# A graph layer's edge gather: more tiles taken from a float32r table on TensorE, fewer by indirect transfer

## The chip, the cores and the metric

The kernel runs on one core of one Trainium2 chip. The metric is the device time of one execution in microseconds (us); it is read from timed runs, and beside them there is one profiled execution. The engines are PE (TensorE), DVE (VectorE), ACT (ScalarE), POOL (GpSimd) and SP (SyncE, which here only issues transfers).

## What is computed

A graph has 3125 nodes with 128 features each (x) and 53125 edges, sorted by their target node (dst), each with 64 features. Cut to what matters:

```
h   = concat([x[src], edge_attr], axis=1)            # 53125 x 192
h   = relu(batchnorm(h @ W1 + b1, g1, be1))          # statistics over all edges
agg = segment_mean(h, dst, 3125)                     # per target node
h2  = relu(batchnorm(concat([x, agg]) @ W2 + b2, g2, be2))
out = layernorm(x + relu(h2 @ Wl + bl))
```

The product is split: `h @ W1` is `(x @ W1x)[src] + edge_attr @ W1e`. The first part is a table of one row per node, of which each edge needs the row of its source node.

## The kernel before

**Phase one** goes over the edges once and keeps every pre-activation row in SBUF (`res`; the fourth group of each cycle goes to DRAM, `spill_out`). A *tile* is 128 edges x 128 features, a *group* is four tiles (q = 0 to 3), a *cycle* (i = 0 to 25) four groups. The node table `x @ W1x` is made at the start, kept in SBUF (`ysb`) and written to DRAM (`ytab`). For every group PE makes the edge product (`product`, L744), GpSimd gathers the table's rows with one indirect transfer per tile (`gather`, L660), and DVE adds the two (`make_h`, L1230). DVE then adds the group to a running sum (`sum_h`, L1251) and ACT's squares of it to another (`sum_sq`, L1258), for the batch norm. Once a cycle DVE makes one-hots of the target nodes (`onehots`, L1209), PE counts them (`counts`, L809), ACT places the counts (`place_counts`, L1012), and in cycles 1 to 14 PE also makes a piece of `x @ W2` (`x_product`, L817), which needs the turned x (`xt0`) in `res`.

**The third group (q = 2) is special.** Two of its four tiles in cycles 2 to 15, and one in cycles 16 to 19, are not gathered but selected on PE: DVE writes one-hots in bfloat16 of which of 3125 nodes each edge wants (`node_onehots`, L1243, five pieces of 125 x 1280 or 125 x 640), PE multiplies 25 blocks of `ysb` in float32 with them (`node_rows`, L757), ACT copies the turned result (`rows_out`, L1039), and PE turns it back onto the edge product (`rows_back`, L765). From cycle 20 all sixteen tiles are gathered.

**Phase two** goes over the kept rows: after the batch-norm chain (L1324 to L1340) DVE takes `max(h, -u)` (`maxes`, L1355), PE sums windows of target nodes with the one-hots (`window_sum`, L890), ACT and GpSimd add them up. It reads the rows from `res` and, for the fourth groups, from DRAM. The node part (`x`, mean, W2, layer norm) follows.

The order of work is written by hand: each engine runs its own list in order and waits on semaphores. GpSimd may start gathering a group once `make_h` of the group four before is done. PE may make a product once `make_h` of the group four before is done. Each transfer of SP's queue waits its turn behind those that stand before it.

Of the kernel before, what the change touches and what calls it, by code (L numbers as in the profile page):

```python
# [27 lines left out]
BF16 = mybir.dt.bfloat16  # L28
I32 = mybir.dt.int32
# [9 lines left out]
U = 4  # L39
# [6 lines left out]
ROWS0 = 2  # L46
ROWS1 = 20
PAIRS1 = 16
NODEQ = 2

def node_tiles(i):

    return 2 if ROWS0 <= i < PAIRS1 else 1 if ROWS0 <= i < ROWS1 else 0

def gnn_kernel(nc, E, x, xt, src, src_rows, dst, dst_rows, ea, W1, b1, g1, be1, W2, b2, g2, be2, Wl, bl, out):
# [8 lines left out]
    YROWS = 25 * P  # L66
# [10 lines left out]
    XLOADS = [BATCH[0:1], BATCH[1:2], BATCH[2:4], BATCH[4:]]  # L77
    YSAVES = [BATCH[0:2], BATCH[2:4], BATCH[4:6], BATCH[6:]]

    ytab = nc.dram_tensor("ytab", (YROWS, F), F32, kind="Internal").ap()  # L80
    h2x_dram = nc.dram_tensor("h2x_dram", (P, H2, N), F32, kind="Internal").ap()
    spill = nc.dram_tensor("spill", (NI, P, TILES * F), F32, kind="Internal").ap()
    rc_dram = nc.dram_tensor("rc_dram", (N,), F32, kind="Internal").ap()
# [3 lines left out]
    with ctx:  # L87
# [9 lines left out]
        GF = TILES * F  # L97
        res = sb("res", [P, NI * KEEP * GF])
# [23 lines left out]
        nodeid = sb("nodeid", [P, NT])[:, :]  # L122
        rowst_sb = sb("node_rows_turned", [P, 2 * P])
# [14 lines left out]
        TAB = 16 * (len(CUTS) * len(YSAVES) + 1)  # L138
# [13 lines left out]
        ysb = tail(NT * F)  # L152
        NODES = range(ROWS0, ROWS1)
        NODEAT = [P * sum(node_tiles(m) for m in range(i)) for i in range(ROWS1 + 1)]
        srcz = tail(NODEAT[-1] // 2).bitcast(BF16)
        TAB0 = at
        xt0 = tail(N)
        XT0 = at
        dsti = tail(TILES * NG)
# [6 lines left out]
        zeros = tail(F)  # L166
# [34 lines left out]
        XP = 20  # L201
        XW = XP * NT
        XSTEPS = [(h, k, min(XP, PN - k)) for k in range(0, PN, XP) for h in range(H2)]
# [12 lines left out]
        psP = [psH[0], psH[1], psT[0], psC[1]]  # L216
# [3 lines left out]
        nodep = psC[0][0:PN, (U + 1) * WIN:(U + 1) * WIN + NT]  # L220
        NODECUT = [(t, t + 5) for t in range(0, NT, 5)]
        NB5 = len(NODECUT)
        NODEROWS = 12
        srcn = res[:, NODEROWS * KEEP * GF:NODEROWS * KEEP * GF + NODEAT[-1]]
        LONE = TAB0 - NT * P
        lone_hot = res[:, LONE:TAB0]
        pair_hot = res[:, LONE - 2 * NT * P:LONE]
        assert LONE - 2 * NT * P >= PAIRS1 * KEEP * GF and LONE >= ROWS1 * KEEP * GF
        assert NODEROWS * KEEP * GF + NODEAT[-1] <= PAIRS1 * KEEP * GF

        def node_chunk(i, b):

            t0, t1 = NODECUT[b]
            w = node_tiles(i) * P
            return (pair_hot if i < PAIRS1 else lone_hot)[0:PN, t0 * w:t1 * w]

        PRODUCTS = [(0, q) for q in range(U)] + [(1, 0)]
        for i in range(1, NI):
            order = [(i, 1), (i, 2), (i, 3)] + ([(i + 1, 0)] if i + 1 < NI else [])
            PRODUCTS += order if i not in NODES else order[1:] + order[:1]  # L240
# [7 lines left out]
        psK = [psT[1], psC[0], psH[0]]  # L248
# [10 lines left out]
        s_srcb = sem("src_rows_spread")  # L259
        s_srcz = sem("src_rows_less_partition")  # L260
# [3 lines left out]
        rows_kept = sem("node_rows_turned_copied")  # L264
        rows_added = sem("node_rows_added")
# [11 lines left out]
        s_zr = sem("zeros_ready")  # L277
# [86 lines left out]
        def slot(i, par, q):  # L364

            return resg(i, q) if q < KEEP else away[par]
# [90 lines left out]
        def _(sp):  # L457
# [1077 lines left out]
```

## Time and profile before

| | |
|---|---|
| timed runs, median of 3 | 635.34 us (634.62 to 635.60) |
| span of the profiled execution (its time on the page; no other time of it is given) | 631.8 us |
| median less span | 3.5 us |
| busy: PE, DVE, ACT, POOL | 503.7, 464.6, 201.2, 403.6 us |
| phase one, up to the first `maxes` | 496.1 us |
| from there to the end | 135.7 us |

The busy times are shares of a span with very different stages, so no engine's total says what bounds it; the section of rows has the stages apart. A float32 matmul stands in the trace as two MATMUL and two LDWEIGHTS instructions; a bfloat16 matmul stands as one each.

### The profile page before, as it was taken

To read this page: it belongs to the slowest core of one execution; us is meant where nothing else is said; L and a number is where in the kernel's file an instruction comes from. 1 tells how busy PE (TensorE), PEld (TensorE's weight loads), DVE (VectorE), ACT (ScalarE), POOL (GpSimd) and SP (SyncE) were. 2 spreads that over 40 slices of the span, in tenths; PEclk is the share of its full clock that TensorE was granted. 3 is DMA by queue.
4 is the path that set the end of the run, shared out by engine and by line. 5 is a ranking of instruction groups with operands and counts; after the bars stand their busy time and mean duration, and the time that the engine had idled before them with its cause. 6 is when DMAs were issued, how large, how long until landed. Compare 5 with 4: busy or idle time off the path is not lost.

```text
span 631.8 us, 9631 instructions
## 1 busy us (share of the span) xinstructions
PE 503.7 (80%) x2681; PEld 412.7 (65%) x2681; DVE 464.6 (74%) x720; ACT 201.2 (32%) x537; POOL 403.6 (64%) x507
## 2 busy tenths in 40 slices
PE   4749999999999999997866634444456899999984
PEld 4637778777777778886664422222223799999674
DVE  4789988888888998987666454454444777777786
ACT  2242222222222222222211211121114566666475
POOL 4777777777777777777777777777777133333500
PEclk9879999999999999999777755555557999999997
DMA  7953344434443434444334342334224277777103
GB/s 202 324 167 121 115 135 135 137 117 138 137 122 116 126 111 138 126 121 121 102 119 121 87 150 78 96 118 121 85 70 120 74 235 228 223 237 231 33 2 101
DMA packets 47608, 84.35 MB, mean 133 GB/s; under 512 B 11721, under 2 KB 23288, under 8 KB 47447
## 3 DMA queue, kind: packets, MB, share of 16 engines
q1 hardware_dynamic: 28834, 47.98, 23.6%
q0 software_dynamic: 12288, 25.19, 15.9%
q10 hardware_dynamic: 6453, 10.79, 4.8%
q8 instruction: 15, 0.25, 0.2%
q14 instruction: 18, 0.15, 0.1%
HBM read 63.82 MB, written 20.08 MB: 133 GB/s over the span
## 4 chain that ended last, share of the span: by engine, by line
PE 53%; POOL 24%; issue 9%; DVE 8%; DMA 3%; ACT 1%; SPq 1%; POOLq 0%; ACTq 0%; DVEq 0%
PE psH L757 25%; POOL res L660 17%; PE psH L890 7%; PE psC L890 7%; POOL work L660 7%; PE psH L744 4%; PE psT L817 3%; PE psT L744 2%; PE psC L744 2%; DVE res L1230 2%; DMA work<-ytab,srci 2%; DVE res L1387 1%; PE psT L809 1%; DMA w1x<-in_L_gnn_W 1%; DVE res L1243 1%
## 5 line engine op out<-in xcount | busy, mean ns | idle before, releaser
L660 POOL DMA_INDIRECT res<-ytab,srci x268 | 253.9, 947 | 81.7 <-issue 79.5
L757 PE MATMUL psH<-res 125*128 125x256 f32 (+1 forms) x900 | 178.7, 359 | 7.0 <-DVE res L1230 7.0
L757 PEld LDWEIGHTS psH<-res 125*128 125x128 f32 x900 | 154.9, 191 | 28.0 <-DVE res L1230 10.7
L660 POOL DMA_INDIRECT work<-ytab,srci x104 | 98.2, 944 | 31.7 <-issue 31.4
L1243 DVE TENSOR_TENSOR res<-res,psC 125x1280 f32<-125x1280 bf16 (+1 forms) x90 | 116.8, 1333 | 0.8 <-ACT res L1030 0.8
L744 PE MATMUL psH<-w1e,work 128*128 128x256 f32 x200 | 69.0, 480 | 42.8 <-DVE res L1230 42.8
L984 ACT ACTIVATE agg<-res 128x512 f32<-128x512 f32 x78 | 49.1, 630 | 143.7 <-DVE res L1230 80.5
L1230 DVE TENSOR_TENSOR res<-psH,res 128x512 f32<-128x512 f32 x50 | 34.5, 689 | 76.5 <-DMA res<-ytab,srci 48.6
L1355 DVE TENSOR_TENSOR work<-res,psX 128x512 f32<-128x512 f32 x103 | 70.2, 687 | 19.5 <-PE psC L890 12.2
L744 PEld LDWEIGHTS psH<-w1e,work 128*128 128x128 f32 x200 | 44.4, 239 | 56.5 <-issue 42.5
L685 POOL TENSOR_TENSOR agg<-agg,srci 128x64 f32 x104 | 32.0, 308 | 70.9 <-ACT srci L1095 70.0
L1258 DVE TENSOR_TENSOR psX<-agg,psX 128x512 f32<-128x512 f32 x103 | 71.0, 689 | 0.0
L1251 DVE TENSOR_TENSOR psS<-res,psS 128x512 f32<-128x512 f32 x78 | 54.3, 696 | 2.7
L890 PE MATMUL psH<-work 128*128 128x128 f32 (+1 forms) x416 | 50.8, 275 | 1.5 <-DVE work L1355 1.5
L890 PE MATMUL psC<-work 128*128 128x128 f32 (+1 forms) x416 | 50.7, 275 | 0.0
L890 PEld LDWEIGHTS psH<-work 128*128 128x128 f32 x416 | 48.5, 192 | 1.9 <-DVE work L1355 1.2
L744 PE MATMUL psC<-w1e,work 128*128 128x256 f32 x100 | 32.7, 458 | 21.0 <-DVE work L1230 21.0
L890 PEld LDWEIGHTS psC<-work 128*128 128x128 f32 x416 | 48.5, 192 | 0.0
L744 PEld LDWEIGHTS psT<-w1e,work 128*128 128x128 f32 x100 | 22.2, 232 | 40.1 <-DVE res L1230 25.0
L744 PE MATMUL psT<-w1e,work 128*128 128x256 f32 x100 | 33.1, 462 | 16.4 <-DVE res L1230 13.4
L744 PEld LDWEIGHTS psC<-w1e,work 128*128 128x128 f32 x100 | 21.5, 226 | 30.0 <-DVE work L1230 27.0
L984 ACT ACTIVATE agg<-work 128x512 f32<-128x512 f32 x25 | 15.7, 630 | 77.5 <-DVE work L1230 77.5
(200 smaller groups left out, 518.7 us busy)
## 6 DMA issues: line engine op xcount, KB each, us to landing
work<-in_edge_attr SPq DMA_DIRECT2D x26, 512.0 KB, 3.7
spill<-work SPq DMA_DIRECT2D x26, 256.0 KB, 2.3
res<-spill SPq DMA_DIRECT2D x25, 256.0 KB, 3.1
res<-ytab,srci POOLq DMA_INDIRECT x268, 2.5
hot_dram<-hotb ACTq DMA_DIRECT2D x13, 256.0 KB, 2.7
hot_dram<-work ACTq DMA_DIRECT2D x13, 256.0 KB, 2.4
hotb<-hot_dram SPq DMA_DIRECT2D x13, 256.0 KB, 2.7
work<-hot_dram SPq DMA_DIRECT2D x13, 256.0 KB, 3.0
```

What stands on the lines that cost most here:

```text
L660: pool.indirect_dma_start(rows[:, j * F:(j + 1) * F], None, ytab, bass.IndirectOffsetOnAxis(ap=srci[:, j, g:g + 1], axis=0)).then_inc(gath ...
L685: pool.tensor_tensor(w, w, wsum[:, q, :], ALU.add).then_inc(agg_added, 1)
L744: last = pe.matmul(psP[q][:, b * 2 * F:(b + 1) * 2 * F], ea_cols(par, q, b), w1e[:, :, :].rearrange("p a f -> p (a f)"), start=(b == 0 or ...
L757: last = pe.matmul(psP[1][:, 0:w], ysb[0:PN, t * F:(t + 1) * F], node_chunk(i, b)[:, k:k + w], start=(t == 0), stop=(t == NT - 1))
L817: pe.matmul(psT[1][:, 0:n * NT].rearrange("o (p t) -> o p t", t=NT), w2x[:, h * P:(h + 1) * P], xtv[:, :, k:k + n].rearrange("f t p -> f p ...
L890: last = pe.matmul(psA[q][:, 0:n], mx[:, q, j * F:(j + 1) * F], hotf[:, q, j * WIN:j * WIN + n], start=(j == 0), stop=(j == TILES - 1))
L984: act.activation(sq[g % 2], slot(i, i % 2, q), ACT.Square).then_inc(sq_ready, 1)
L1230: dve.tensor_tensor(h, psP[q][:, :], h, ALU.add).then_inc(h_ready, 1)
L1243: dve.tensor_tensor(node_chunk(i, b).rearrange("p (t e) -> p t e", t=t1 - t0), srcz[0:PN, NODEAT[i]:NODEAT[i] + w].unsqueeze(1).broadcast_ ...
L1251: last = dve.tensor_tensor(psS[:, :], slot(i, par, q), psS[:, :], ALU.add)
L1258: last = dve.tensor_tensor(psX[:, :], sq[g % 2], psX[:, :], ALU.add)
L1355: dve.tensor_tensor(tiles(mx[:, q, :]), tiles(hin), negu, ALU.max).then_inc(m_ready, 1)
```

## The change

All four tiles of the third group are now selected on PE, in every cycle from 2 to 25; twelve of sixteen tiles are gathered. The table is laid out as 112 partitions x 28 rows (3136 rows, node = 28 p + t) and kept in two float32r halves: `tab_hi` is ACT's copy of `ysb`, `tab_lo` is `ysb - tab_hi`, made by DVE (`table_low`). A node number is split in three: its upper part names one of 112 x 7 cells of four rows (SPAN = 4, STEPS = 7), its lower two bits one of the four. The upper parts (`srcr`, keys) are made by DVE, written to DRAM, and spread over 112 partitions per cycle (`load_keys`). For each tile DVE compares 112 x 896 (`node_onehot`), PE runs 14 matmuls of 512 moving columns (7 steps x high and low, `node_tile`), which leave all four candidate rows of each edge in one PSUM bank, ACT copies the first (`node_first`), and DVE overwrites it where the edge wants the second, third or fourth (`node_pick`, three predicated copies of 128 x 128). Tiles of cycle i + 1 are selected during cycle i.

PSUM: two banks hold edge products (`psP`) where four did, so `product` waits for `make_h` of the group two before; two banks hold candidates (`psN`).

SBUF: the halves and one-hots lie where the rows of cycles 18 to 25 were. These go into the place of cycles 0 to 7 (`home`), whose rows are first written to `spill_all` (8 x 768 KB) and, when the last pick is done, read back by SP (`back_all`); DVE waits for all of it before phase two. `place` gives the cycle's place in phase two.

```diff
+            def load_keys(i):
+                if i - 2 in NODES:
+                    sp.wait_ge(nhot_ready, node_nth(i - 2, NODET - 1) + 1)
+                sp.dma_start(keys[i % 2][0:TP, :], key_dram[i - NODE0, :].partition_broadcast(TP)
+                             ).then_inc(keys_in[i % 2], 16)
...
+                if i < SWAP:
+                    sp.dma_start(spill_all[i, :, :], res[:, i * KEEP * GF:(i + 1) * KEEP * GF]).then_inc(spilled_all, 16)
...
+            sp.wait_ge(node_rows, (SPAN - 1) * NODEALL)
+            sp.wait_ge(spilled_all, 16 * SWAP)
+            for i in range(SWAP):
+                k = place(i, NI) * KEEP * GF
+                sp.dma_start(res[:, k:k + KEEP * GF], spill_all[i, :, :]).then_inc(back_all, 16)
...
-                for j in range(node_tiles(i) if q == NODEQ else 0, TILES):
+                for j in range(NODET if q == NODEQ and i in NODES else 0, TILES):
...
-                pe.wait_ge(h_ready, g - U + 1)
+                pe.wait_ge(h_ready, g - 1)
...
+            def node_tile(i, j):
+                n = node_nth(i, j)
+                pe.wait_ge(nhot_ready, n + 1)
+                if n >= 2:
+                    pe.wait_ge(node_rows, (SPAN - 1) * (n - 1))
+                for a in range(STEPS):
+                    k = (j * STEPS + a) * P
+                    for part, table in enumerate((tab_hi, tab_lo)):
+                        last = pe.matmul(psN[n % 2][:, :], nhot[0:TP, k:k + P],
+                                         table[0:TP, a * SPAN * F:(a + 1) * SPAN * F],
+                                         start=(a == 0 and part == 0), stop=(a == STEPS - 1 and part == 1))
+                last.then_inc(nhot_used, 1)
...
+                act.wait_ge(nhot_used, n + 1)
+                act.activation(node_slot(i, j), psN[n % 2][:, 0:F], ACT.Copy).then_inc(first_of_four, 1)
...
+                dve.tensor_tensor(nhot[0:TP, j * STEPS * P:(j + 1) * STEPS * P].rearrange("p (a e) -> p a e", a=STEPS),
+                                  keys[i % 2][0:TP, j * P:(j + 1) * P].unsqueeze(1).broadcast_to([TP, STEPS, P]),
+                                  nodep.unsqueeze(2).broadcast_to([TP, STEPS, P]), ALU.is_equal).then_inc(nhot_ready, 1)
...
+                dve.copy_predicated(node_slot(i, j), pick[:, b - 1, j, place(i, NI):place(i, NI) + 1].broadcast_to([P, F]),
+                                    psN[n % 2][:, b * F:(b + 1) * F]).then_inc(node_rows, 1)
...
+                    dve.tensor_tensor(tab_lo[0:TP, cut], ysb[0:TP, cut], tab_hi[0:TP, cut].bitcast(F32), ALU.subtract
+                                      ).then_inc(s_lo, 1)
...
+            dve.wait_ge(back_all, 16 * SWAP)
```

PE's list, in one cycle of the middle (cycle 11) before; `psH <- res` at L757 is `node_rows`, with five pieces of five matmuls:

```order
239 L757 MATMUL psH<-res 128x256 [waits node_onehots_ready]
240 L757 MATMUL psH<-res 128x256 x4
241 L757 MATMUL psH<-res 128x256 [waits node_onehots_ready]
242 L757 MATMUL psH<-res 128x256 x4
243 L817 MATMUL psT<-res,agg 128x500 [waits cnt_rows_placed]
244 L744 MATMUL psT<-w1e,work 128x256 [waits h_ready]
...
246 L744 MATMUL psC<-w1e,work 128x256 [waits h_ready]
...
248 L744 MATMUL psH<-w1e,work 128x256 [waits h_ready,ea_loaded1]
...
250 L809 MATMUL psT<-hotb,onesb 128x256 [waits w2_x_copied,cnt_rows_placed,hotb_ready]
...
252 L744 MATMUL psH<-w1e,work 128x256 [waits h_ready,node_rows_turned_copied]
...
254 L765 MATMUL psT<-ident,node_rows_turned 128x128 [waits node_rows_turned_copied]
```

The same list after the change, from the third product of a middle cycle on; behind row 412 stand the 28 matmuls of two tiles (rows 413 to 440), and 14 each stand behind 442 and 458:

```order
406 L863 MATMUL psT<-res,agg 128x504 [waits cnt_rows_placed]
407 L792 MATMUL psH<-w1e,work 128x256 [waits h_ready]
...
409 L855 MATMUL psT<-hotb,onesb 128x256 [waits w2_x_copied,cnt_rows_placed,hotb_ready]
...
411 L792 MATMUL psT<-w1e,work 128x256 [waits h_ready,ea_loaded1]
412 L792 MATMUL psT<-w1e,work 128x256
...
441 L792 MATMUL psH<-w1e,work 128x256 [waits h_ready]
442 L792 MATMUL psH<-w1e,work 128x256
...
457 L792 MATMUL psT<-w1e,work 128x256 [waits h_ready]
458 L792 MATMUL psT<-w1e,work 128x256
```

The selection now stands in four pieces between the products, and the first product of the next cycle stands behind the counts and ahead of the last two tiles.

DVE's list before, from the third group of a middle cycle to the next cycle's first; L1243 is `node_onehots`:

```order
294 L1227 TENSOR_TENSOR res<-psT,res 128x256 [waits node_rows_added,gathered1_2,ea_product_ready]
295 L1228 COPY res<-psT 128x256
296 L1251 TENSOR_TENSOR psS<-res,psS 128x512 [waits h_ready]
297 L1258 TENSOR_TENSOR psX<-agg,psX 128x512 [waits squares_ready]
298 L1243 TENSOR_TENSOR res<-res,psC 125x640 [waits node_onehots_used]
299 L1230 TENSOR_TENSOR work<-psC,work 128x512 [waits gathered1_3,ea_product_ready]
300 L1251 TENSOR_TENSOR psS<-work,psS 128x512 [waits h_ready]
301 L1258 TENSOR_TENSOR psX<-agg,psX 128x512 [waits squares_ready]
302 L1243 TENSOR_TENSOR res<-res,psC 125x640 [waits node_onehots_used] x2
303 L1230 TENSOR_TENSOR res<-psH,res 128x512 [waits gathered0_0,ea_product_ready]
```

DVE's list after, from the fourth group (`make_h` at L1291) to the next cycle's first; L1314 is `node_pick`, L1302 `node_onehot`:

```order
403 L1291 TENSOR_TENSOR work<-psH,work 128x512 [waits gathered1_3,ea_product_ready]
404 L1328 TENSOR_TENSOR psS<-work,psS 128x512 [waits h_ready]
405 L1314 COPY_PREDICATED res<-res,psH 128x128 [waits node_rows_picked,node_rows_first_of_four]
406 L1335 TENSOR_TENSOR psX<-agg,psX 128x512 [waits squares_ready]
407 L1314 COPY_PREDICATED res<-res,psH 128x128 [waits node_rows_picked,node_rows_first_of_four]
408 L1302 TENSOR_TENSOR node_onehots<-res,psC 112x896 [waits node_onehots_used]
409 L1314 COPY_PREDICATED res<-res,psH 128x128 [waits node_rows_picked,node_rows_first_of_four]
410 L1302 TENSOR_TENSOR node_onehots<-res,psC 112x896 [waits node_onehots_used]
411 L1314 COPY_PREDICATED res<-res,psC 128x128 [waits node_rows_picked,node_rows_first_of_four] x3
412 L1302 TENSOR_TENSOR node_onehots<-res,psC 112x896 [waits node_onehots_used]
413 L1291 TENSOR_TENSOR res<-psT,res 128x512 [waits gathered0_0,ea_product_ready]
```

Three one-hots and six picks now stand between the sums of the fourth group and the next cycle's first `make_h`, where two pieces of one-hots stood.

## Rows read from the trace of the kernel before

**Rows 1.** The page: busy time and share of each engine.

```profile
PE 503.7 (80%) x2681; PEld 412.7 (65%) x2681; DVE 464.6 (74%) x720; ACT 201.2 (32%) x537; POOL 403.6 (64%) x507
```

**Rows 2.** The page's groups by line: busy, mean ns, idle before.

```profile
L660 POOL DMA_INDIRECT res<-ytab,srci x268 | 253.9, 947 | 81.7 <-issue 79.5
L660 POOL DMA_INDIRECT work<-ytab,srci x104 | 98.2, 944 | 31.7 <-issue 31.4
```

**Rows 3.** Windows: length, busy time per engine, PE clock, DMA share, GB/s.

```profile
47.00:290.00 243.00, 238.25 (x1071) 193.76 (x1072) 219.27 (x267) 60.62 (x142) 183.88 (x195) 1.00 0.42 126
400.00:488.00 88.00, 44.08 (x99) 24.52 (x97) 41.05 (x60) 18.86 (x45) 66.44 (x71) 0.54 0.33 97
496.00:591.00 95.00, 93.57 (x836) 93.44 (x836) 73.31 (x108) 55.63 (x206) 31.67 (x103) 1.00 0.70 207
```

**Rows 4.** Timeline of PE, one middle cycle: start, duration, instruction.

```profile
205.53 11.06 PE L757 MATMUL psH<-res 125*128 125x256 f32 x50 [0.34 <-DVE res L1230]
216.42 2.04 PE L817 MATMUL psT<-res,agg 128*128 128x500 f32 x2
218.28 1.05 PE L744 MATMUL psT<-w1e,work 128*128 128x256 f32 x4
...
220.89 0.60 PE L809 MATMUL psT<-work,onesb 128*128 128x256 bf16 x4
221.33 1.03 PE L744 MATMUL psH<-w1e,work 128*128 128x256 f32 x4
...
223.14 11.06 PE L757 MATMUL psH<-res 125*128 125x256 f32 x50 [0.34 <-DVE res L1230]
```

**Rows 5.** Timeline of DVE in the same cycle.

```profile
204.78 0.69 DVE L1230 TENSOR_TENSOR res<-psH,res 128x512 f32<-128x512 f32 x1 [1.65 <-PE psH L744]
205.51 0.70 DVE L1251 TENSOR_TENSOR psS<-res,psS 128x512 f32<-128x512 f32 x1
206.11 0.69 DVE L1258 TENSOR_TENSOR psX<-agg,psX 128x512 f32<-128x512 f32 x1
206.71 1.22 DVE L1209 TENSOR_TENSOR work<-psC,loc 128x1024 bf16<-128x1024 f32 x1
207.84 0.41 DVE L1227 TENSOR_TENSOR res<-psT,res 128x256 f32<-128x256 f32 x1
...
209.82 1.48 DVE L1243 TENSOR_TENSOR res<-res,psC 125x1280 f32<-125x1280 bf16 x1
211.22 0.68 DVE L1230 TENSOR_TENSOR work<-psC,work 128x512 f32<-128x512 f32 x1
```

**Rows 6.** Timeline: copies of 128 columns out of PSUM on two engines.

```profile
296.78 0.28 ACT L1039 ACTIVATE node_rows_turned<-psH 128x128 f32<-128x128 f32 x1
...
310.83 0.28 DVE L1228 COPY res<-psT 128x128 f32<-128x128 f32 x1
```

**Rows 7.** Timeline of DVE: first groups of cycles 2 and 25, last group, phase two.

```profile
57.34 0.68 DVE L1230 TENSOR_TENSOR res<-psH,res 128x512 f32<-128x512 f32 x1
...
475.22 0.69 DVE L1230 TENSOR_TENSOR res<-psH,res 128x512 f32<-128x512 f32 x1 [3.07 <-DMA res<-ytab,srci]
...
490.32 0.69 DVE L1230 TENSOR_TENSOR work<-psC,work 128x512 f32<-128x512 f32 x1 [1.19 <-DMA work<-ytab,srci]
...
496.13 1.88 DVE L1355 TENSOR_TENSOR work<-res,psX 128x512 f32<-128x512 f32 x3 [0.52 <-PE psX L878]
```

**Rows 8.** Windows with busy DMA engines (last two columns: DMA share, GB/s).

```profile
9.00:13.00 4.00, 4.00 (x19) 4.00 (x20) 2.47 (x6) 0.99 (x2) 2.92 (x3) 1.00 0.97 333
...
28.00:30.00 2.00, 2.00 (x15) 1.82 (x14) 1.97 (x4) 0.63 (x1) 1.39 (x3) 1.00 1.05 420
...
505.00:585.00 80.00, 80.00 (x718) 80.00 (x718) 61.72 (x91) 48.87 (x180) 27.39 (x90) 1.00 0.77 230
```

**Rows 9.** The page's DMA issues: size, us from issue to landing.

```profile
spill<-work SPq DMA_DIRECT2D x26, 256.0 KB, 2.3
```

More of the change, by code:

```diff
@@ L28 @@
 BF16 = mybir.dt.bfloat16
+F32R = mybir.dt.float32r
 I32 = mybir.dt.int32
@@ L97, in gnn_kernel, with shared @@
         GF = TILES * F
+        AREA = (NI - SWAP) * KEEP * GF
+        with ExitStack() as low:
+            def shared(name, cols, dt=F32R):
+                return low.enter_context(nc.sbuf_tensor(name, [P, cols], dt))
+            shared("below_node_area", AREA, F32)
+            tab_hi = shared("table_high", TT * F)
+            tab_lo = shared("table_low", TT * F)
+            nhot = shared("node_onehots", NODET * STEPS * P)
         res = sb("res", [P, NI * KEEP * GF])
@@ L150, in tail @@
             return res[:, at:at + n]
[L152 to L157, printed above, removed]
+        NODES = range(NODE0, NI)
+        keys = [tail(NODET * P) for _ in range(2)]
+        pick = tail((SPAN - 1) * NODET * NI).bitcast(I32).rearrange("p (b j s) -> p b j s", b=SPAN - 1, j=NODET)
+        assert at >= AREA + 2 * TT * F + NODET * STEPS * P
+        at = AREA
+        xt0 = tail(YROWS)
         XT0 = at
+        ysb = tail(TT * F)
+        srcr = tail(NODET * P)[0:len(NODES), :]
+        low2 = tail(NODET * NI).bitcast(I32).rearrange("p (j s) -> p j s", j=NODET)
         dsti = tail(TILES * NG)
@@ L761, in rows_back @@
-            def rows_back(i):
-                pe.wait_ge(rows_kept, i - ROWS0 + 1)
-                for j in range(node_tiles(i)):
-                    last = pe.matmul(psP[NODEQ][:, j * F:(j + 1) * F], rowst_sb[:, j * P:(j + 1) * P], ident[:, :],
-                                     start=False, stop=(j == node_tiles(i) - 1))
-                last.then_inc(rows_added, 1)
+            def node_tile(i, j):
+                if i not in NODES or j >= NODET:
+                    return
+                n = node_nth(i, j)
+                pe.wait_ge(nhot_ready, n + 1)
+                if n == 0:
+                    pe.wait_ge(s_hi, len(YBATCH))
+                    pe.wait_ge(s_lo, len(YBATCH))
+                if n >= 2:
[7 more added lines that the diff above has]
+                last.then_inc(nhot_used, 1)
@@ L859, in stay_awake @@
                 for _ in range(n):
[L860 removed]
+                    pe.matmul(psC[1][:, 0:P], ident[:, :], ident[:, :], start=True, stop=True)
             stay_awake(3)
```

343 lines of the change are left out of this document (190 added, 153 removed).

## The prediction

> **What bounds the kernel now.** I read the page's busy times first [rows 1]: no engine is near the whole span, so the stages must be told apart. The windows do that [rows 3]: from 47 to 290 us PE is busy 238 of 243 us at the full clock, from 400 to 488 us half of the time at 0.54 of it, and in phase two again nearly always. GpSimd's gathers are the other candidate: 372 of them to the table, each about 0.945 us long with 0.30 us of issue before it [rows 2], (253.9 + 81.7) / 268 = 1.252 us each, 465 us in all, one after the other. So the number of gathered tiles sets the cycle wherever PE is not slower: 14 tiles make 17.5 us, 15 make 18.8, 16 make 20.0. In cycles 2 to 14 PE needs just as long: its period is 223.14 - 205.53 = 17.61 us with 0.34 us idle [rows 4]. Both engines are at the limit there; afterwards GpSimd alone is, and it is the sum of both that the span shows: from the first `make_h` of cycle 2 to that of cycle 25, 475.22 - 57.34 = 417.9 us, 18.2 per cycle [rows 7]. After that come 20.9 us to the first `maxes` at 496.13 (the last four groups' gathers, then the batch-norm chain, 5.8 us behind the last `make_h` at 490.32), then 135.7 us of phase two and the node part.
>
> **GpSimd.** 96 tiles leave its list where 32 had, so 64 transfers go. Twelve tiles make 15.0 us per cycle. It may run four groups ahead of `make_h` as before, so if another engine is slower than 15.0, GpSimd waits and costs nothing.
>
> **PE.** Per cycle 56 matmuls of 512 columns in float32r come in; `node_rows` and `rows_back` go. No row shows float32r. The nearest rows: a float32 matmul of 256 columns is two instructions of 10.89 / 50 = 0.218 us [rows 4], so 0.87 us for 512 columns; bfloat16 takes 0.44 / 4 = 0.110 us for 256 columns, so 0.22 for 512. Below 0.22 lies nothing, since both come to one column per cycle of the full clock (a float32 matmul then being four passes). The bounds are 0.22 and 0.87; I take 0.218, one pass, because the kernel multiplies by a high and a low half itself, which is what several passes would do inside. Loads of 128 columns stay hidden: in phase two PE alternates load and half matmul 836 times each in 95 us, 0.114 us a pair [rows 3], well under 0.218.
> So a tile takes 14 x 0.218 = 3.05 us and four take 12.2. With four products at 2.61 / 3 = 0.87, the counts 0.44 and the piece of `x @ W2` 1.86 [rows 4] that is 12.2 + 3.5 + 0.4 + 1.9 = 18.0 us in cycles 1 to 12, and 16.1 from cycle 15 on (13 and 14 have a short piece). PE is slower than the gathers throughout.
>
> **DVE.** Spacings rather than durations count, since instructions overlap by about 0.09 us [rows 5]: 0.73 for `make_h` with the wait of `sum_h` on it, 0.60 each for the sums, 1.13 for the 1024-element one-hots. Per cycle that is 4 x 1.93 + 1.13 = 8.85. The five pieces of 1280 (211.22 - 209.82 = 1.40 each) leave. Four of 896 elements come: 1.40 x 896 / 1280 = 0.98, say 1.0 each, 4.0. Twelve predicated copies of 128 columns come, which no row shows: a plain copy of that size lasts 0.28 [rows 6], 0.20 spaced; if the mask or the old value costs a second reading it is 0.33 spaced, and twice over 0.45. I take 0.20 to 0.27 (it moves the same elements as the plain copy) and add 0.13 where a pick waits on the one before (the last three, and a few others). That is 2.4 to 3.2 plus 0.6. In sum DVE works about 16.2 us a cycle, against 8.85 + 7.0 = 15.9 before: more, and now with a hand-over in both directions at each tile.
>
> **How the two meet.** I lay the lists side by side with t = 0 at the end of a cycle's last tile on PE. PE: product 0.9, tile 3.9, product 4.8, tile 7.9. DVE cannot pick before ACT's copy of 0.28 [rows 6], so its first pick starts at 4.4; then pick, sum, pick, sum, pick and the one-hots, 2.9 us, bring it to 7.3, `make_h` of the second group is done at 8.0, of the third at 10.0. PE's fourth product waits for the one and the next cycle's first for the other. With the x piece PE is at 9.7 by itself and needs neither wait: the two tiles end at 18.0, period 18.1. Without it PE waits until 8.1 and 10.1, makes products and counts to 11.0, and the tiles end at 17.1: period 17.2. From cycle 2 to cycle 25 that makes 11 x 18.1 + 12 x 17.2 = 405.5, less about 2 because cycle 24 makes no one-hots: 403.5 us, against 417.9. **14.4 us are gained.**
>
> **The start.** Seven pieces of `table_high` on ACT, seven of `table_low` at 0.60, 4.2 us, and four one-hots, 4.0, fall into cycle 0 of DVE, and some 3.4 us of short list work ahead of it. Much hides behind the twenty gathers up to cycle 1's end (25 us of GpSimd), but PE's first tile waits for the low half. Followed through, the first `make_h` of cycle 2 comes at about 60 instead of 57.3: **2.7 us lost** (bounds 0 and 8). The 8 writes of 768 KB hide in cycles whose DMA share is 0.42 [rows 3]; the two row moves (keys) are small and come a cycle early.
>
> **The read-back.** It starts only at the last pick, just ahead of the first `make_h` of cycle 25. 8 x 786 KB = 6.29 MB. With all engines busy the trace moves 333 to 420 GB/s [rows 8]; in phase two, with smaller rows, 230 at 0.77. I take 360: 17.5 us, plus 2 of latency (a 256 KB write needs 2.3 to land [rows 9]), plus 0.6 because the first one-hots stand behind it in SP's queue: `maxes` 20 us after cycle 25's first `make_h`. What else must happen there: 10 us for the groups now that gathers wait ready, counts and folds beside it, the products of the last group with itself, the chain: about 18.5. So the read-back ends last, by little, and the tail is 20 against 20.9. **0.9 us gained**, of which I give 0.8 to a colder start of PE. Phase two does the same work, 135.7.
>
> **The sum.** 60 + 403.5 + 20 + 0.8 + 135.7 = 620 us of span, against 631.8; with the 3.5 us between span and median, **624 us**.
>
> **Rivals.**
> *DVE becomes the bound (slower, 0.18).* Place: the predicated copies. DVE's cycle is 13.5 + 12 c; with c over 0.38 it passes PE's 18.1. At 0.45 the cycle is about 18.3 to 19.1, and the lists followed through give 26 us more, 650. It decides against the change from about 0.36 on. For it: no such instruction is in the trace, and it has three operands. Against it: TENSOR_TENSOR with two operands is no slower per element than COPY [rows 5, 6].
> *Hand-overs cost more than I gave them (slower, 0.10).* Each tile passes PE, ACT, DVE and back; another 0.7 us per cycle is 16 us, 640. Speaking for it: products have half the PSUM they had.
> *float32r needs two or four passes (slower, 0.06).* 1344 matmuls at 0.436 give about 905 us, at 0.87 about 1490.
> *The read-back is slow (0.07).* At 230 GB/s it takes 27.4 us, 10 more: 634, about no change.
> *PE is faster than its columns (faster, 0.03).* If consecutive matmuls of 512 columns overlapped, PE and DVE would fall under GpSimd's 15.0 us; 23 cycles of that are 345 instead of 403.5, 566 us. Against it stands that bfloat16 comes at one column per clock in rows 4; DVE's 16.2 forbids half of it too, leaving some 595.
> The Trainium skill (TensorE: Matmul & The Clock Gate, Back-to-back issue gap) gives about 131 ns per 512-column matmul as sustained; the trace's 0.110 us for 256 columns disagrees.
> *My forecast* has the rest, 0.56, from 614 to 633.
>
> **Chances and range.** A measurement of this kernel can tell some 0.2%, 1.3 us. Faster: 0.56 + 0.03 + 0.03 of the slow read-back, 0.62. Same: the other 0.04 of it. Slower: 0.18 + 0.10 + 0.06 = 0.34. The range 613 to 650 leaves out the passes, PE's overlap and the worst of DVE.
>
> **What would show it.** L810 MATMUL spaced 0.218 us; L1314 at 0.28 to 0.35 long; 1.25 us gathers with idle before them "<-DVE"; periods of 18.1 and 17.2; DVE's first `maxes` released by DMA `spill_all`. Wrong if L1314 is over 0.45, if PE shows gaps over 1.5 us per cycle, or if L810 is not one pass.

## The result, and the profile after

The changed kernel takes 643.01 us (median of 4 runs, 642.42 to 644.37), the kernel before 634.98 us (634.38 to 635.60) on the same chip: a ratio of 1.0133, 95% interval 1.0117 to 1.0149. It is slower by 8.0 us, where the prediction had it faster by 11; 643 lies inside the range of 613 to 650, on the side that was held less likely. The profiled execution took 643.24 us, its span is 641.5.

The page of the changed kernel: busy times, the chain that ended last by engine, and the costliest groups (to be held against [rows 1] and [rows 2]):

```profile
PE 591.4 (92%) x3067; PEld 485.9 (76%) x3067; DVE 510.9 (80%) x1015; ACT 215.3 (34%) x621; POOL 344.3 (54%) x442
...
PE 76%; DVE 14%; issue 4%; DMA 3%; ACT 1%; SPq 1%; DVEq 0%; ACTq 0%; POOL 0%; POOLq 0%
...
L709 POOL DMA_INDIRECT res<-ytab,srci x204 | 193.0, 946 | 111.8 <-DVE res L1291 53.7
...
L1302 DVE TENSOR_TENSOR node_onehots<-res,psC 112x896 fp32r<-112x896 f32 x96 | 103.4, 1079 | 0.0
L1314 DVE COPY_PREDICATED res<-res,psH 128x128 f32<-128x128 int32 x144 | 42.7, 296 | 59.8 <-ACT res L1087 59.7
```

GpSimd lost 59 us of work and now idles "<-DVE res L1291", that is, for `make_h`; it stands with 0% on the chain. PE gained 88 us of work and holds 76% of the chain. Windows of the changed kernel (length, busy time per engine, PE clock, DMA share, GB/s) say where:

```profile
60.00:290.00 230.00, 229.25 (x978) 177.86 (x976) 187.73 (x356) 58.80 (x159) 139.94 (x148) 1.00 0.47 145
300.00:480.00 180.00, 175.54 (x780) 141.36 (x780) 152.86 (x293) 42.42 (x122) 116.26 (x124) 1.00 0.39 114
...
490.00:495.00 5.00, 4.90 (x25) 3.22 (x25) 2.72 (x5) 4.43 (x7) 0.00 (x0) 1.00 1.01 424
495.00:500.00 5.00, 4.06 (x37) 3.87 (x36) 2.15 (x12) 3.67 (x5) 0.00 (x0) 1.00 1.01 415
500.00:505.00 5.00, 0.69 (x3) 0.50 (x4) 1.15 (x3) 1.03 (x3) 0.00 (x0) 0.82 0.48 180
505.00:510.00 5.00, 5.00 (x25) 5.00 (x25) 4.46 (x6) 1.06 (x4) 0.62 (x2) 0.50 0.38 107
```

PE is busy 229.25 of 230 us where there are pieces of `x @ W2`, and 175.5 of 180 us in the later cycles, where before it had half of its time free [rows 3]. The span, stage by stage (us; the starts are those of DVE's `make_h` and of the first `maxes`; the forecast's 0.8 for a colder PE is put to phase two):

| stage | before | forecast | after |
|---|---|---|---|
| up to the first `make_h` of cycle 2 | 57.3 | 60 | 63.05 |
| from there to that of cycle 25 | 417.9 | 403.5 | 418.8 |
| from there to the first `maxes` | 20.9 | 20 | 22.1 |
| phase two and the node part | 135.7 | 136.5 | 137.6 |
| span | 631.8 | 620 | 641.5 |

The 418.8 us are eleven cycles of 18.43 on average (2 to 12; one is 18.78 and the next 18.08), one of 17.56, one of 23.73 (cycle 14), nine of 17.54 to 17.64 and a last one of 16.54. Three pieces of the timeline carry the rest. PE at the start of a middle cycle's tiles, in the changed kernel:

```profile
202.07 0.39 PE L810 MATMUL psH<-table_high,node_onehots 112*128 112x512 f32 x1
202.30 0.40 PE L810 MATMUL psH<-table_low,node_onehots 112*128 112x512 f32 x1
...
204.81 0.39 PE L810 MATMUL psC<-table_high,node_onehots 112*128 112x512 f32 x1
...
207.99 1.03 PE L792 MATMUL psH<-w1e,work 128*128 128x256 f32 x4
```

Float32r is one pass: from 204.81 to 207.99 fourteen matmuls take 3.18 us, 0.227 each (the 0.39 us of each overlap). Cycle 14, all engines:

```profile
288.98 0.54 PE L863 MATMUL psT<-res,agg 128*128 128x112 f32 x2
289.56 0.28 ACT L1087 ACTIVATE res<-psH 128x128 f32<-128x128 f32 x1 [8.24 <-PE psT L863]
...
289.87 0.30 DVE L1314 COPY_PREDICATED res<-res,psH 128x128 f32<-128x128 int32 x1 [5.81 <-ACT res L1087]
...
290.30 0.94 POOL L709 DMA_INDIRECT res<-ytab,srci x1 [8.08 <-PE psT L863]
...
293.53 2.08 PE L792 MATMUL psH<-w1e,work 128*128 128x256 f32 x4 [4.01 <-DVE res L1291]
```

The last piece of `x @ W2` reads the turned x from the place in `res` that cycle 15's rows take next. It stands on PE behind two tiles. ACT's first copy of the next cycle, every pick behind it and GpSimd's gathers wait 8 us for it, and PE in its turn 4.0 us. The wait costs more than itself, for behind it PE works at the lower clock (0.50 in this window):

```profile
295.00:297.00 2.00, 2.00 (x8) 1.45 (x7) 2.00 (x6) 0.40 (x2) 1.40 (x2) 0.50 0.34 57
```

From 293.53 to the next tile's start at 297.61 two products and the counts take 4.1 us, where at the full clock and without a wait they take 2.1. Of the 6.1 us by which this cycle is longer than its neighbours some 3.6 are the longer wait and some 2.5 the clock. And the end of phase one, DVE and SP's queue:

```profile
481.83 0.68 DVE L1291 TENSOR_TENSOR res<-psT,res 128x512 f32<-128x512 f32 x1
...
499.92 0.16 DVE L1432 TENSOR_TENSOR col<-col 128x1 f32<-128x1 f32 x1
...
503.92 1.88 DVE L1448 TENSOR_TENSOR work<-res,psX 128x512 f32<-128x512 f32 x3 [3.85 <-DMA spill<-work]
```
```profile
481.95 4.24 SPq L555 DMA_DIRECT2D res<-spill_all  x8
...
494.99 0.35 SPq L511 DMA_DIRECT2D spill<-work  x1
```

The chain is ready at 500.07, 18.2 us behind cycle 25's first `make_h`, as forecast (18.5). Then `maxes` waits 3.85 us, and what comes last is not the read-back but the last ordinary 256 KB write of `spill_out`: `maxes` overwrites `work`, from which it is read. The last read-back, the three loads that SP issued behind it and the write, with the time from issue to landing:

```profile
res<-spill_all SPq DMA_DIRECT2D x1, 768.0 KB, 15.4
hotb<-hot_dram SPq DMA_DIRECT2D x1, 256.0 KB, 11.4
work<-spill SPq DMA_DIRECT2D x1, 256.0 KB, 11.6
work<-hot_dram SPq DMA_DIRECT2D x1, 256.0 KB, 11.8
spill<-work SPq DMA_DIRECT2D x1, 256.0 KB, 8.5
```

Issued at 485.56, 490.25, 490.64, 491.11 and 494.99, they land at 500.95, 501.6, 502.3, 502.9 and 503.5. So the last read-back is there 0.9 us after the chain is ready; the other 2.6 us are the loads and the write that land behind it. PE starts after 4.31 us of idling at a granted clock of 0.50, which is the lower level, 1.2 GHz; its first 16 matmuls of phase two last 3.67 us.

### The profile page after: what moved, and what is told of

Same layout as the page of the kernel before. It is cut to its first block, busy times and chain, and to the rows that moved or that the text cites. A ratio compares the mean times of both kernels' runs of the same rounds, so it can differ in the third digit from the quotient of the medians.

```text
span 641.5 us, 11124 instructions
## 1 busy us (share of the span) xinstructions
PE 591.4 (92%) x3067; PEld 485.9 (76%) x3067; DVE 510.9 (80%) x1015; ACT 215.3 (34%) x621; POOL 344.3 (54%) x442
## 4 chain that ended last, share of the span: by engine, by line
PE 76%; DVE 14%; issue 4%; DMA 3%; ACT 1%; SPq 1%; DVEq 0%; ACTq 0%; POOL 0%; POOLq 0%
PE psH L810 24%; PE psC L810 18%; PE psH L933 8%; PE psC L933 7%; PE psT L792 6%; PE psH L792 5%; PE psT L863 3%; DVE res L1291 2%; DVE psX L1335 2%; DVE res L1314 2%; DMA spill<-work 1%; DVE work L1273 1%; PE psT L855 1%; DVE res L1480 1%; DVE hotb L1273 1%
## 5 line engine op out<-in xcount | busy, mean ns | idle before, releaser
L709 POOL DMA_INDIRECT res<-ytab,srci x204 | 193.0, 946 | 111.8 <-DVE res L1291 53.7
L810 PE MATMUL psH<-table_high,node_onehots 112*128 112x512 f32 x336 | 142.2, 423 | 4.6 <-DVE table_low L1322 4.6
L810 PE MATMUL psC<-table_high,node_onehots 112*128 112x512 f32 x336 | 135.5, 403 | 0.0
L810 PE MATMUL psH<-table_low,node_onehots 112*128 112x512 f32 x336 | 132.7, 395 | 0.0
L810 PE MATMUL psC<-table_low,node_onehots 112*128 112x512 f32 x336 | 131.0, 390 | 0.0
L1302 DVE TENSOR_TENSOR node_onehots<-res,psC 112x896 fp32r<-112x896 f32 x96 | 103.4, 1079 | 0.0
L1314 DVE COPY_PREDICATED res<-res,psH 128x128 f32<-128x128 int32 x144 | 42.7, 296 | 59.8 <-ACT res L1087 59.7
L810 PEld LDWEIGHTS psH<-table_high,node_onehots 112*128 112x128 f32 x336 | 64.3, 191 | 18.4 <-issue 5.0
L810 PEld LDWEIGHTS psH<-table_low,node_onehots 112*128 112x128 f32 x336 | 64.4, 192 | 13.4
L810 PEld LDWEIGHTS psC<-table_low,node_onehots 112*128 112x128 f32 x336 | 63.2, 188 | 13.1
L810 PEld LDWEIGHTS psC<-table_high,node_onehots 112*128 112x128 f32 x336 | 63.1, 188 | 13.1
```

The source lines that it names most:

```text
L709: pool.indirect_dma_start(rows[:, j * F:(j + 1) * F], None, ytab, bass.IndirectOffsetOnAxis(ap=srci[:, j, at:at + 1], axis=0)).then_inc(ga ...
L810: last = pe.matmul(psN[n % 2][:, :], nhot[0:TP, k:k + P], table[0:TP, a * SPAN * F:(a + 1) * SPAN * F], start=(a == 0 and part == 0), stop ...
L1302: dve.tensor_tensor(nhot[0:TP, j * STEPS * P:(j + 1) * STEPS * P].rearrange("p (a e) -> p a e", a=STEPS), keys[i % 2][0:TP, j * P:(j + 1) ...
L1314: dve.copy_predicated(node_slot(i, j), pick[:, b - 1, j, place(i, NI):place(i, NI) + 1].broadcast_to([P, F]), psN[n % 2][:, b * F:(b + 1) ...
```

## The experiments

Ratios are to the kernel before, on the same chip, with 95% intervals. Stages are read from the timeline as above.

**The x piece ahead of the tiles (e1_x_first).**

```diff
             def edge_step(i, par, nth):
+                if i == len(XSTEPS):
+                    x_product(i - 1)
                 product(i, par, nth, 1)
                 node_tile(i + 1, 0)
...
-                if i <= len(XSTEPS):
+                if i < len(XSTEPS):
                     x_product(i - 1)
```

> The last piece of x @ W2 (cycle 14) is made before that cycle's tiles instead of between the second tile and the third product. Theory A (ACT's first copy for cycle 15 and GpSimd's gathers for it wait for this piece, and that is the extra 6.2 us of the 23.73 us cycle in the changed kernel's trace): that cycle falls to 17.6, the time by 6 us, from 643 to 637. Rival (the long cycle comes from the clock of TensorE, which fell there, or from a late transfer, and the wait only stands beside it): the cycle stays above 22 us, the time at 642 to 644.

638.20 us (636.18 to 638.68), ratio 1.0064 (1.0046 to 1.0082). Cycle 14 takes 18.0 us instead of 23.7, and the other cycles do not move: the later ones stay at 17.6. The granted clock stays at 1.00 there (from 281 to 301 us), so its fall in the changed kernel came of the wait and was not the cause of the long cycle. PE now meets 0.45 us of waiting there instead of 4.01:

```profile
289.02 1.13 PE L792 MATMUL psH<-w1e,work 128*128 128x256 f32 x4
...
291.04 1.10 PE L792 MATMUL psT<-w1e,work 128*128 128x256 f32 x4 [0.45 <-DVE res L1293]
```

So some 5 of the 8 us by which the change lost are one wait, which stands in the diff's order and which I had not followed.

**The read-backs later, waited for later (e2_late_wait).** SP issues them behind the loads for phase two, and DVE waits for them only ahead of the 18th cycle of phase two, the first that needs one.

```diff
+            sp.wait_ge(node_rows, (SPAN - 1) * NODEALL)
...
+                sp.dma_start(res[:, k:k + KEEP * GF], spill_all[i, :, :]).then_inc(back_all, 16)
             spill_out(NI - 1, 1)
...
-                with dve.Fori(2, NI) as i:
+                with dve.Fori(2, NI - SWAP) as i:
+                    sum_step(i)
+                dve.wait_ge(back_all, 16 * SWAP)
+                with dve.Fori(NI - SWAP, NI) as i:
                     sum_step(i)
```

> The eight read-backs stand behind the first loads of phase two in SP's queue, and VectorE waits for them only before the 18th cycle of phase two, which is the first that needs them. Theory A (VectorE's 3.9 us wait for them, and the clock that falls in the idle time of TensorE before phase two, are all that they cost): first maxes at about 500.3 instead of 503.9, phase two at 135.7 instead of 137.6, in sum 5 us less: 638. Rival (their 6.3 MB cost as much wherever they lie, because phase two's own loads need the same transfer engines): phase two gets longer by 4 to 15 us, and the time stays at 642 or goes to 650.

648.83 us (646.83 to 649.84), ratio 1.0234 (1.0213 to 1.0255): slower by 6 us than the change itself. Theory A fell; the time lies where the rival had it, but not for the rival's reason, since phase two takes 137.0 us and the loss stands ahead of it. SP's queue and DVE in this kernel:

```profile
487.28 5.42 SPq L613 DMA_DIRECT2D res<-spill_all  x8
494.73 0.33 SPq L511 DMA_DIRECT2D spill<-work  x1
508.08 1.88 DVE L1447 TENSOR_TENSOR work<-res,psX 128x512 f32<-128x512 f32 x3 [8.26 <-DMA spill<-work]
```

The read-backs are issued 5.3 us later than in the change, and the 256 KB write lands 4.2 us later. The write is what `maxes` waits for. Whether the write is held by the queue's order or by busy DMA engines this run can't tell.

**The start in pieces (e3_pieces).** PE's first tile waits for each piece of the two halves, not for all.

```diff
-                if n == 0:
-                    pe.wait_ge(s_hi, len(YBATCH))
-                    pe.wait_ge(s_lo, len(YBATCH))
...
+                    if n == 0:
+                        pe.wait_ge(s_hi, a + 1)
+                        pe.wait_ge(s_lo, a + 1)
```

> TensorE's first tile waits for the low half of the table piece by piece, one of seven before each step, instead of for all seven. Theory A (the start is late because this tile begins at 40.3 us, 5 us after the first piece): it begins at about 36.5, the first make_h of cycle 2 comes at 59 to 60 instead of 63.05, time 640. Rival (VectorE's own list of 8 us, table_low and one-hots, sets the start): make_h of cycle 2 moves by under 1 us, time 642 to 643.

641.13 us (640.34 to 642.19), ratio 1.0109 (1.0088 to 1.0131). PE's first tile, in the changed kernel and in this one:

```profile
40.30 0.76 PE L810 MATMUL psH<-table_high,node_onehots 112*128 112x512 f32 x1 [4.58 <-DVE table_low L1322]
40.86 0.63 PE L810 MATMUL psH<-table_low,node_onehots 112*128 112x512 f32 x1
```
```profile
37.64 0.76 PE L810 MATMUL psH<-table_high,node_onehots 112*128 112x512 f32 x1 [0.88 <-DVE table_low L1322]
```

From cycle 0's first `make_h` to cycle 2's it takes 34.6 us (27.26 to 61.84) instead of 36.8 (26.22 to 63.05). That is 2.2 us less, and `make_h` of cycle 2 itself comes 1.2 us earlier, between what theory A and the rival had. The other runs that leave the start as the change has it take 35.8 to 36.8 us for this stretch; of the runs with this edit three take 34.6 and one (e8) 36.7. So the edit is worth some 1 to 2 us, but not in every execution. The medians differ by 1.9 us, the ratios by 1.5, and their intervals overlap.

**Half of PE's columns (e4_no_low).**

```diff
-                    for part, table in enumerate((tab_hi, tab_lo)):
+                    for part, table in enumerate((tab_hi,)):
```

> Leaves out the low half of the table: 7 instead of 14 matmuls per tile, so the selected rows are float32r-rounded. VectorE's and GpSimd's lists are untouched. Theory A (TensorE's list of 18.4 us is what a cycle lasts; behind it stands VectorE with about 16.2, then GpSimd with 15.0): TensorE needs 28 x 0.227 = 6.4 us less, cycles fall to 16.2, time about 598. Rival B (the chain tile, first copy, picks, next tile sets the cycle, whose length has more hand-overs than matmuls): cycles fall by 1 us at most, time above 620.

579.41 us (577.68 to 584.00), ratio 0.9150 (0.9102 to 0.9198). Most cycles take 15.33 us, below my 16.2 (cycle 14 takes 19.6), and the window shows what then bounds them:

```profile
257.00:410.00 153.00, 115.04 (x480) 85.15 (x480) 149.69 (x289) 45.07 (x122) 112.85 (x120) 0.98 0.45 134
```

DVE is busy 149.7 of 153 us, PE 115. So the limit of DVE's list is at most 15.3 us, not the 16.2 of the working, and in the changed kernel DVE has 2 to 3 us to spare in each cycle: PE was the bound.

**One predicated copy of three (e5_one_pick).** Two of the three `node_pick` of each tile are left out, and the counts that wait for them follow.

```diff
+PICKS = 1
...
-                if i not in NODES or j >= NODET:
+                if i not in NODES or j >= NODET or b < SPAN - PICKS:
```

> Leaves out two of the three predicated copies of every tile (the second and third candidate row are never taken), so 8 of 12 go per cycle; everything else stands. Theory A (TensorE's list is the bound): cycles 2 to 12 stay at 18.4, the later ones lose the waits of TensorE for make_h, 17.56 to about 17.0, time 634 to 640. Rival B (VectorE's list with its hand-overs is the bound): each cycle loses 8 x 0.2 = 1.6 us and the dependent waits, time about 605.

630.66 us (628.80 to 631.96), ratio 0.9939 (0.9918 to 0.9960). The cycles with an x piece stay at 18.43 to 18.44 us; the later ones go from 17.56 to 16.65. The window of later cycles:

```profile
325.00:425.00 100.00, 100.00 (x458) 83.26 (x457) 82.57 (x127) 24.98 (x72) 68.05 (x73) 1.00 0.44 125
```

PE is never idle there: 16.65 us is what its list takes by itself in a cycle without an x piece. In the first stretch PE alone sets the time in the changed kernel too; in the second its waits in the hand-overs between PE, ACT and DVE add 0.9 us. The time is below theory A's 634 because the later cycles lose 0.9 us instead of 0.6 and cycle 14 loses 2.3. The copies themselves last 0.295 us, as forecast; three that wait on one another take 1.10, which is 0.40 from one to the next, where the forecast had 0.33.

**Three tiles instead of four (e6_three).**

```diff
-NODET = 4
+NODET = 3
```

> Three tiles of the third group come from the table on TensorE instead of four, and GpSimd gathers thirteen of sixteen (one number changed, NODET = 3). Theory A (TensorE at 18.4 is the bound and has to lose a tile, 3.2 us): TensorE 15.2, VectorE 16.1 - 1.0 - 0.8 = 14.3, GpSimd 13 x 1.248 = 16.2, so cycles of 16.2 to 16.5 set by GpSimd, 23 of them 2 us shorter at the first eleven and 1.2 at the rest: time about 643 - 36 = 607, faster than the kernel before. Rival B (hand-overs set the cycle): the share of GpSimd's extra tile and the hand-overs add up, cycles above 17.3, time 630 or more.

596.43 us (595.79 to 597.66), ratio 0.9401 (0.9383 to 0.9419): 6% faster than before, and better than theory A's 607. Its gathers and a window of its later cycles:

```profile
L709 POOL DMA_INDIRECT res<-ytab,srci x228 | 215.4, 945 | 69.5 <-issue 66.7
```
```profile
320.00:430.00 110.00, 96.37 (x418) 74.00 (x416) 90.45 (x169) 27.52 (x75) 83.06 (x88) 1.00 0.43 124
```

Idle ahead of the gathers is nearly all issue again: GpSimd runs through, thirteen tiles at 1.25 make 16.2 us, and the cycles average (432.8 - 61.57) / 23 = 16.14. Cycle 14 still takes 21.3 us, but GpSimd gathers on during it, and the three cycles behind it take 14.5 to 14.8. The fourth tile costs PE 3.18 us (fourteen matmuls) and saves GpSimd 1.25, which it can't use. That is where the change's gain went.

**All three edits together, with four tiles (e8_four_all) and with three (e7_three_all).** They are e1, e2 and e3 in one kernel.

> Four tiles as in the change, with the same three edits. Theory A (the three costs are independent and are what I missed beside the slower matmul spacing): 643 - 6 - 5 - 3 = 629, which is faster than the kernel before at 635. Rival (they overlap, or a later wait takes their place): 636 or more, no faster than before.

> Three tiles, with the early last piece of x @ W2, the late wait for the read-back and the piecewise wait at the start. Theory A: what the single edits give adds to what three tiles give, less what GpSimd's list hides (its start is fixed by the gathers, so the piecewise wait gives little): about 607 - 6 - 5 = 596. Rival: the edits give nothing once GpSimd is the bound, 605 or more.

Four tiles: 639.69 us (639.33 to 642.68), ratio 1.0086 (1.0069 to 1.0103), where the rival had it. Three: 599.85 us (599.01 to 600.17), ratio 0.9454 (0.9437 to 0.9471), slower than e6 by 3.4, between the two theories. Cycle 25's first `make_h` comes 3.2 us earlier than in e6 (429.56 against 432.8), but the first `maxes` 31.0 us behind it, with 6.37 us of wait for `spill<-work`, where e6 has 27.1 and no such wait. The late read-backs of e2 cost more than the two other edits bring.

**The read-backs from another queue (e9_own_queue).**

```diff
-                sp.dma_start(res[:, k:k + KEEP * GF], spill_all[i, :, :]).then_inc(back_all, 16)
...
+                pool.dma_start(res[:, k:k + KEEP * GF], spill_all[i, :, :]).then_inc(back_all, 16)
```

> The changed kernel with one thing altered: the eight read-backs are issued from GpSimd's queue behind its last gather of phase one, no longer from SP's, and DVE waits for them only ahead of the 18th cycle of phase two. Theory A (the order of SP's queue held phase two back: the last group's write to DRAM, which the first maxes needs, stands behind the read-backs in that queue): first maxes some 18.3 us behind cycle 25's first make_h, at about 500.3 instead of 503.9, phase two again 135.7 us instead of 137.6, the whole 637 to 638 us. Rival (bandwidth: the 6.3 MB cost the same from any queue): first maxes at 503 or later, or phase two longer by as much, 642 us or more.

643.11 us (641.99 to 644.78), ratio 1.0149 (1.0127 to 1.0172): my theory fell. As in e2, DVE waits for the read-backs only ahead of the 18th cycle of phase two. GpSimd issues the eight at 481.36, the write is issued at 494.13 in SP's queue, where only 256 KB loads stand ahead of it, and `maxes` still waits:

```profile
502.73 1.88 DVE L1447 TENSOR_TENSOR work<-res,psX 128x512 f32<-128x512 f32 x3 [3.51 <-DMA spill<-work]
```
```profile
490.00:495.00 5.00, 4.90 (x30) 3.70 (x29) 1.98 (x3) 4.70 (x7) 0.00 (x0) 1.00 1.01 413
495.00:500.00 5.00, 3.56 (x30) 3.17 (x28) 2.23 (x12) 3.83 (x7) 0.00 (x0) 1.00 1.03 413
```

The DMA engines are fully busy, whichever queue feeds them, and every transfer of SP's queue is slow beside the read-backs: its three loads of 256 KB, issued from 487.23 to 488.09, take 6.7, 8.8 and 11.7 us to land, the last of them at 499.8, and the write lands at 502.3. What the write would do with neither read-backs nor loads ahead of it in its queue was not tried.

**Four and three tiles with e1, e3 and e9 (e10_four_best, e11_three_best).**

> Four tiles as in the changed kernel, with the three waits taken out that single runs priced: the last piece of x @ W2 ahead of the tiles (5.7 us), the first tile starting on the first pieces of the table (2.2 us), the read-backs on GpSimd's queue and waited for late (5 us). Theory A (the three are separate and add up): 643.0 - 12.9 = about 630 us, 4 to 5 us faster than before. Rival (they overlap, or a saved start is lost to PE's work later on): 636 us or more, slower than before.

> The same as the kernel with all three edits, but three selected tiles a cycle. Theory A (the edits' places, start, cycle 14 and read-back, are the same with three tiles): 596.4 less some 8 us, 587 to 590 us. Rival (with three tiles GpSimd sets the cycle and takes up what PE gains at the start and in cycle 14, and its read-backs wait behind later gathers): 595 us or more.

Four tiles: 634.61 us (633.78 to 636.50, 10 runs), ratio 1.0013 (1.0000 to 1.0026), between theory A's 630 and the rival's 636. Against the change's span, 8.6 us are gone: 1.7 at the start, 5.6 between cycles 2 and 25, 0.6 up to `maxes` and 0.7 of phase two; the 4 us of the read-back are missing from the sum, for the reason of e9. Three tiles: 595.88 us (593.98 to 596.37), ratio 0.9386 (0.9367 to 0.9404), level with e6. Its start is 3.1 us shorter, but cycles 2 to 25 take 370.6 against 371.2 us, since GpSimd sets them, and phase two 138.1 instead of 136.0 us; ahead of it `maxes` waits 2.65 us for `spill<-work`, where e6 has none of that. With three tiles the rival was right.

**The read-backs spread over phase two (e12_spread; with e1 and e3 and four or three tiles e13_four_spread, e14_three_spread).**

```diff
                 for i in range(4, 10):
                     load_step(i, i % 2)
+                    read_back(i - 2)
```

> The changed kernel with one thing altered: the eight read-backs are issued in phase two, one behind each of the loads of its cycles 2 to 9, so that none of them is under way while the last group's write to DRAM is; DVE waits for them ahead of the 18th cycle of phase two. Theory A (the 256 KB write is late because the read-backs keep all DMA engines busy, from whichever queue they come): the write lands in some 2.4 us again, first maxes some 18.3 us behind cycle 25's first make_h, phase two 135.7 to 137 us, the whole 637.5 to 639.5 us. Rival (the read-backs then crowd out phase two's own loads: 786 + 524 KB per cycle of 3.57 us would be 367 GB/s): phase two 4 us or more longer, 642 us or more.

> Four tiles with the x piece first, the start in pieces, and the read-backs spread over phase two. Theory A (adds up): 634.6 less 3.2 and less some 1 us of phase two, 630 to 631 us, faster than before by 0.5%. Rival (phase two's loads crowded out): 634 us or more.

> The same with three selected tiles a cycle. Theory A: 595.9 less 2.6 us of wait ahead of the first maxes and less 2 us of phase two, 591 to 592 us. Rival (GpSimd's last gathers, not the write, set the first maxes; phase two crowded out): 595 us or more.

646.50 us (645.61 to 648.20), ratio 1.0204 (1.0180 to 1.0228). DVE of e12 at the start of phase two and some cycles into it, and a window of that stretch:

```profile
500.75 1.88 DVE L1454 TENSOR_TENSOR work<-res,psX 128x512 f32<-128x512 f32 x3 [0.52 <-PE psX L928]
...
535.25 0.69 DVE L1454 TENSOR_TENSOR work<-res,psX 128x512 f32<-128x512 f32 x1 [1.45 <-DMA res<-spill]
...
545.36 0.69 DVE L1454 TENSOR_TENSOR work<-res,psX 128x512 f32<-128x512 f32 x1 [2.42 <-DMA res<-spill]
```
```profile
511.00:545.00 34.00, 28.29 (x245) 27.48 (x243) 20.54 (x31) 14.88 (x60) 9.14 (x30) 1.00 0.95 345
```

With no read-back under way the write is in time: `maxes` is released by the chain itself, 18.8 us behind cycle 25's first `make_h` (481.99), and PE's first 16 matmuls take 2.00 us at full clock. Together with e9 that gives the cause of the 3.85 us: the load that the read-backs put on the DMA engines, from whichever queue. The rival holds as well: phase two is 143.1 us, 7.4 longer than before's 135.7, its own loads standing in DMA engines that are 0.95 busy. e13 gives 642.56 us (638.88 to 643.97), ratio 1.0141 (1.0117 to 1.0164), e14 601.72 us (600.95 to 605.38), ratio 0.9508 (0.9474 to 0.9543), both slower than with the read-backs ahead of phase two, as the rivals had it. With four tiles the 6.3 MB cost 3 us or more wherever I put them. With three tiles they cost time too, in another place. In e6 the write is not late, since it is issued when the read-backs are through, but the last gathers are. DVE's `make_h` of cycle 25's second group and the landing of the last gathers into `res` in e6 (the first two lines), and the gathers in e14:

```profile
438.98 0.69 DVE L1291 TENSOR_TENSOR res<-psH,res 128x512 f32<-128x512 f32 x1 [4.16 <-DMA res<-ytab,srci]
res<-ytab,srci POOLq DMA_INDIRECT x6, 6.3
```
```profile
res<-ytab,srci POOLq DMA_INDIRECT x6, 2.5
```

Cycle 24's first `make_h` stands at 414.10 in e6 and at 414.30 in e14; the first `maxes` follows 45.8 us later in e6 and 38.7 us later in e14, which has no read-backs there. These 7.1 us e14 pays back in phase two, which takes 146.0 us instead of 136.0. A slower rate in phase two, one in two cycles, was not tried.

## Why the prediction was wrong

Its mechanism was right in the main: PE becomes the bound, GpSimd falls off the path (0% of the chain), float32r is one pass, the predicated copies last what the lower bound said. The forecast gain was 14.4 us in 417.9, and it was lost in the places below; the span came out 21.5 us over the 620 of the sum. The steps that failed are the price of a tile on PE, the irregular cycle 14, and what was left out beside the read-back.

1. **"How the two meet", the period of 18.1 and 17.2 us.** They are 18.43 and 17.56. The term that was mis-sized is the tile: 512 columns are spaced 0.227 us, not 0.218, which is 56 x 0.009 = 0.5 us a cycle on the bounding engine. Some 0.2 of it came back: the x piece takes less than the 1.86 reckoned, and in the later cycles the hand-overs cost 0.9 us (17.56 against e5's 16.65) where the working had 1.1 (17.2 against 16.1). That is +3.7 us over eleven cycles, +3.7 over ten later ones, and +1.3 in the last, which I had at 15.2 and is 16.54. So the rival of the hand-overs did not come true; they were a little cheaper than I had them.
2. **The same step, what stands at cycle 14.** I counted 13 and 14 as cycles with "a short piece". That the last piece of `x @ W2` had come to stand behind two tiles, and that cycle 15's rows need its place, is in the diff and in the order of the lists, and I looked at a middle cycle only. +6.5 us over the 17.2 (e1 gets 5.7 back), of which some 2.5 are the lower clock behind the wait. It is the largest miss in one place.
3. **"The start", 2.7 us lost.** 5.7 were (63.05 against 57.34), within my bounds of 0 and 8; some 1 to 2 of them because the first tile waits for all fourteen pieces of the halves (e3). That tile also runs at the lower clock, 5.9 us from 40.30 to 46.16 instead of 3.2, which the working had at nothing; what of it reached cycle 2 no run separates.
4. **"The read-back ends last, by little": 20 us to the first `maxes`.** 22.1, and phase two 1.1 us longer. The read-backs themselves came as reckoned: the last lands at 500.95, 19.1 us behind cycle 25's first `make_h`. "The first `maxes` released by `spill_all`" did not come true, for I left out what is on the way beside them: the last group's own write, which DVE's first `maxes` needs, took 8.5 us where its kind takes 2.4. My next guess, the order of SP's queue alone, was wrong too (e9); it is the load on the DMA engines (e9 and e12). Of the 1.1 us in phase two the colder start of PE is the greater part: 3.67 us instead of 2.00 for its first 16 matmuls, 1.7, where I had given 0.8.
5. **"3.5 us between span and median".** In every run, before and after, the profiled run's own time is 1.7 to 1.9 us over its span. The 3.5 mixed the profiled execution's luck with it. Here the median is 1.5 us over the span: -2.0 us, the only error to the other side, which by chance made the total look better than its parts.

3.0 + 15.3 + 2.1 + 1.1 make the 21.5 us. Against them stood a forecast gain of 11.8 us of span (631.8 less 620); items 1 and 2 alone, 15.3 us, turn its sign. With items 2 and 3 mended and part of 4 the change is level with before (e10, 1.0013), so the gain of four tiles is about nothing even then: PE's 18.4 and 17.6 us per cycle against the 18.2 that before had on average. That PE would be slower than the gathers "throughout" stood in the prediction as a fact about the bound; it was in truth the reason why the fourth tile could not pay. Three tiles balance the engines (PE 18.43 - 3.18 = 15.3 us, DVE at most that, GpSimd 16.2) and give 596 us, the best of these kernels.

The Trainium skill (TensorE: Matmul & The Clock Gate, Back-to-back issue gap) gives about 131 ns per sustained 512-column matmul. The prediction set that aside for the trace of before; the 0.227 us here disagree with it as well.

## What to carry over

When work moves from one engine to another, compute both engines' period per unit moved and stop where they cross: the tile by which GpSimd could no longer set the pace cost PE 3.2 us a cycle. Follow the first, the last and every irregular cycle through the new lists, not only a middle one; a read of a buffer that has moved behind other work holds everyone who wants the buffer next. A bulk transfer "beside" the critical path must be priced by what it does to the small transfers that are on it; here a write and, in e6, the gathers were late while the DMA engines were full, whichever queue carried the bulk.

## What the runs showed of the hardware

A float32r matmul of 112 rows, 128 stationary and 512 moving columns comes every 0.227 us at the granted clock of 1.00 (every 0.43 us at the start, at the lower level). A predicated copy of 128 x 128 from PSUM with a broadcast int32 mask lasts 0.295 us, has the next instruction 0.20 behind it, and is spaced 0.40 where each waits for the one before. While eight reads of 768 KB in rows of 6 KB from DRAM are under way, the DMA engines move 413 to 424 GB/s in all; a 256 KB write issued among them lands after 8.5 us (2.4 is the median of its kind), and a gather of 128 rows after 6.3 us instead of 2.5. After 4.3 us without work PE's first 16 matmuls of phase two took 3.67 us, after 1.0 us 2.00.
